# Attention over heads in a six-block network on one Trainium2 core: split real and imaginary parts, gates without matmuls, mixing by features in two token halves

## The chip, the cores and the metric

The program runs on one core of a Trainium2 chip. A core has TensorE (PE in the profile; PEld is its weight loads), VectorE (DVE), ScalarE (ACT), GpSimd (POOL) and SyncE (SP, whose queue starts the DMAs). The metric is device time in microseconds (us); lower is better.

## What is computed

Two levels of three residual blocks (cross attention, attention, feed forward) act on x, 8 x 64 tokens of 512 features. The change touches one of the six: the attention over heads of level 1, between cross attention and experts. In a token its 8 heads attend to each other; there is no attention between tokens. Cut to what matters:

```python
x = x + attn(layernorm(x))
q, k, v = split(query @ W_qkv.T + b_qkv)               # each [B, S, 8 heads, 64]
encode(v) = v / max(norm(v), 1e-12) * exp(1j * phases) # phases: one per feature
for depth in range(3):                                 # on encode(q) and encode(k)
    s1, s2 = state[:, :, :-1], state[:, :, 1:]         # heads i and i + 1
    rot = cos(theta / 2) * s2 + sin(theta / 2) * exp(1j * phi) * conj(s2)
    state = concat([abs(s1)**2 * rot + (1 - abs(s1)**2) * s2, state[:, :, -1:]])
coh = exp(1j * angle(sum(encode(v), heads)))
for c in range(4):                                     # circuits
    pattern = einsum('bsid,bsjd->bsij', conj(qa), ka)  # 8 x 8 in each token
    probs = softmax(abs(pattern)**2 * scale)
    co = einsum('bsij,bsjd->bsid', sqrt(probs + 1e-12), encode(v)) * coh
    final += sup_w[c] * clip(abs(co), 1e-6, 1) * exp(1j * angle(co))
return real(final).reshape(B, S, 512) @ W_out.T + b_out
```

## The kernel before

Everything is one program whose blocks follow one another. Each block is made of stages (class `Stage`, L59), and each stage ends with a barrier over all engines, which the profile lists as L73. In a stage every engine has its own instruction list, in the order written; lists meet only at semaphores. All tensors of this block are fp32, 512 tokens; a PSUM bank holds 512 columns.

`head_attention` (L1708) opens a stage for its long-lived tensors and calls, in this order:

`norm_transpose` (L92): layer norm on VectorE, transposes on TensorE (L192), copies to `xt`. SyncE loads `w_qk` meanwhile (L1737), in which the columns of each head stand twice.

`head_project` (L1749): for each of 16 queries and keys (`u`), four matmuls of 512 columns (L1822) whose 128 output rows are the head's 64 features twice, for the real and the imaginary part; ScalarE adds the bias (L1863) and squares (L1868); a matmul sums the squares over the 64 rows (L1812). Then the values, head by head, 64 rows (L1836), transposed to (head, token) groups (L1842). VectorE inverts the 16 x 512 lengths (L1947), splits them into three bf16 parts (L1951, L1954), TensorE spreads them over the rows (L1851), and VectorE scales the states with them and with the cosine or sine of the phase (L1963). It also builds 21 gate matrices `rot` (L1923, L1926). GpSimd makes the constant matrices first and TensorE waits for them (`made`).

`entangle` (L1970): `units` is 3 depths x 7 gates x (query, key) = 42. For each, ScalarE squares head i (L1991), TensorE adds real and imaginary squares (L2010, matrix `same`) and applies the gate (L2013, matrix `rot`), ScalarE copies the first result (L2000), VectorE multiplies (L2024) and adds (L2026).

`head_scores` (L2031): tokens lie in 32 groups of 16 (`NG`, `GT`). TensorE turns the keys (L2070) and multiplies query group by key group, 128 x 128 (L2063), of which only equal tokens count; VectorE picks these with a mask `own` (L2094) and sums (L2099).

`head_mix` (L2106): softmax on small tensors (L2156 to L2166, exponential L2256, root L2267). Then, for 4 token tiles x 4 circuits in two halves each (`halves`, 32): VectorE or, for each fourth, GpSimd widens the weights to 128 x 128 blocks (L2145), TensorE transposes them (L2312), ScalarE copies (L2281), TensorE multiplies them with the values, 64 columns at a time (L2324). ScalarE takes size and sign (L2274, L2275), VectorE clips and scales (L2174 to L2177), GpSimd adds over the circuits (L2206, L2208) and makes `face` (L2227 to L2240), VectorE applies it (L2183, L2184). At the end the sums are transposed (L2344, L2288), and TensorE makes the output with 8 matmuls of 64 rows and a bias matmul for each token tile (L2353, L2354), VectorE adds it to x (L2197).

## Time and profile before

| | us |
|---|---|
| Median of 3 runs (lowest, highest) | 3393.12 (3390.45, 3395.27) |
| The profiled execution | 3391.88 |
| Its span, first to last instruction | 3390.2 |
| TensorE busy in it | 3130.2 (92%) |
| VectorE busy | 1574.2 (46%) |
| ScalarE busy | 1010.7 (30%) |
| GpSimd busy | 133.7 (4%) |

The profile is of one execution, 1.7 us longer than its span. "Busy" is the time in which an engine executes; TensorE's matmuls are pipelined, so that busy is not the same as at its peak. The clock column (PEclk) is the TensorE clock that was granted, as a share of 2.4 GHz; 0.50 is the lower of its two levels. An fp32 matmul shows as two records. `out<-in` names what an instruction writes and reads; the prefix is the stage (n, hp, he, hs, hm) or `ha` for the tensors of the whole block.

### The profile page before, as it was taken

To read this page: it belongs to the slowest core of one execution; us is meant where nothing else is said; L and a number is where in the kernel's file an instruction comes from. 1 tells how busy PE (TensorE), PEld (TensorE's weight loads), DVE (VectorE), ACT (ScalarE), POOL (GpSimd) and SP (SyncE) were. 2 spreads that over 40 slices of the span, in tenths; PEclk is the share of its full clock that TensorE was granted. 3 is DMA by queue.
4 is the path that set the end of the run, shared out by engine and by line. 5 is a ranking of instruction groups with operands and counts; after the bars stand their busy time and mean duration, and the time that the engine had idled before them with its cause. 6 is when DMAs were issued, how large, how long until landed. Compare 5 with 4: busy or idle time off the path is not lost. (4 is left out here: it accounts for less than half of the span.)

```text
span 3390.2 us, 41575 instructions
## 1 busy us (share of the span) xinstructions
PE 3130.2 (92%) x17509; PEld 1704.9 (50%) x17517; DVE 1574.2 (46%) x1808; ACT 1010.7 (30%) x1527; POOL 133.7 (4%) x239
## 2 busy tenths in 40 slices
PE   6979999959899999899999999999999869779899
PEld 3334444424344444466666666666666523348353
DVE  5359999955532222334343434343333240679110
ACT  3354333313332222223232323232332202344010
POOL 1000000000000000000000000000000000016000
PEclk9989999989999999999999999999999979795599
DMA  5123343333233333445554555455544420000113
GB/s 199 50 78 90 93 140 92 93 138 112 87 112 101 102 100 108 148 95 138 119 141 109 139 119 141 109 137 118 141 112 98 90 94 0 0 13 1 53 47 136
DMA packets 467232, 338.50 MB, mean 100 GB/s; under 512 B 227780, under 2 KB 432901, under 8 KB 462375
## 3 DMA queue, kind: packets, MB, share of 16 engines
q1 hardware_dynamic: 467046, 335.84, 36.0%
q8 instruction: 139, 2.28, 0.3%
q14 instruction: 47, 0.38, 0.0%
HBM read 227.68 MB, written 53.58 MB: 83 GB/s over the span
## 5 line engine op out<-in xcount | busy, mean ns | idle before, releaser
L366 PE MATMUL vw_pv<-vw_wv,vw_ctx 128*128 128x512 f16 (+1 forms) x1296 | 497.0, 384 | 63.0 <-DVE vw_vst L386 27.6
L367 PE MATMUL vw_pv<-vw_wv,vw_ctx 128*128 128x512 f16 (+1 forms) x1296 | 496.9, 383 | 0.0
L368 PE MATMUL vw_pv<-vw_wv,vw_ctx 128*128 128x512 f16 (+1 forms) x1296 | 495.9, 383 | 0.0
L1442 PE MATMUL ca_p_s<-early_halves,ca_qw 128*128 128x448 f16 (+2 forms) x1408 | 467.4, 332 | 1.4 <-DVE ca_qw L1555 1.4
L1443 PE MATMUL ca_p_s<-early_halves,ca_qw 128*128 128x448 f16 (+2 forms) x1408 | 467.4, 332 | 0.0
L1444 PE MATMUL ca_p_s<-early_halves,ca_qw 128*128 128x448 f16 (+2 forms) x1408 | 467.3, 332 | 0.0
L1555 DVE TENSOR_TENSOR ca_qw<-ca_p_w,ca_qw 128x512 f16<-128x512 f32 x128 | 88.5, 691 | 545.6 <-ACT ca_qw L1505 545.6
L386 DVE TENSOR_TENSOR vw_vst<-vw_pv,vw_vst 128x512 f16<-128x512 f32 x162 | 110.7, 687 | 377.1 <-ACT vw_vst L377 377.0
L1505 ACT ACTIVATE ca_qw<-ca_p_w 128x512 f16<-128x512 f32 x128 | 76.4, 597 | 560.5 <-PE ca_p_w L1423 560.5
L366 PEld LDWEIGHTS vw_pv<-vw_wv,vw_ctx 128*128 128x128 f16 (+1 forms) x1296 | 127.8, 99 | 229.3 <-issue 40.4
L377 ACT ACTIVATE vw_vst<-vw_pv 128x512 f16<-128x512 f32 x162 | 95.4, 592 | 468.6 <-PE vw_pv L368 468.6
L1444 PE MATMUL ca_p_s<-ca_ctx,ca_qw 128*128 128x448 f16 (+2 forms) x640 | 215.5, 337 | 0.0
L1443 PE MATMUL ca_p_s<-ca_ctx,ca_qw 128*128 128x448 f16 (+2 forms) x640 | 215.4, 337 | 0.0
L1442 PE MATMUL ca_p_s<-ca_ctx,ca_qw 128*128 128x448 f16 (+2 forms) x640 | 215.4, 337 | 0.0
L368 PEld LDWEIGHTS vw_pv<-vw_wv,vw_ctx 128*128 128x128 f16 (+1 forms) x1296 | 127.8, 99 | 156.8 <-issue 6.5
L367 PEld LDWEIGHTS vw_pv<-vw_wv,vw_ctx 128*128 128x128 f16 (+1 forms) x1296 | 127.7, 99 | 154.5 <-issue 7.7
L1444 PEld LDWEIGHTS ca_p_s<-early_halves,ca_qw 128*128 128x128 f16 x1408 | 138.0, 98 | 99.4 <-issue 0.9
L1442 PEld LDWEIGHTS ca_p_s<-early_halves,ca_qw 128*128 128x128 f16 x1408 | 138.0, 98 | 90.9 <-DVE ca_qw L1555 1.7
L1513 ACT ACTIVATE ca_probs<-ca_p_s,ca_small 128x896 f32<-128x896 f32 (+1 forms) x128 | 117.7, 925 | 220.3 <-DVE ca_small L1564 220.3
L1443 PEld LDWEIGHTS ca_p_s<-early_halves,ca_qw 128*128 128x128 f16 x1408 | 138.0, 98 | 89.1 <-issue 0.7
L1577 DVE SCALAR_TENSOR_TENSOR ca_parts<-ca_probs,ca_small,ca_parts 128x1602 f16<-128x1602 f32 x64 | 120.8, 1888 | 119.1 <-ACT ca_parts L1522 119.1
L873 ACT ACTIVATE work<-early_halves,mb_a_neg 128x252 f32<-128x252 f32 x256 | 104.7, 492 | 218.0 <-DVE ms_h L905 215.4
(405 smaller groups left out, 5126.4 us busy)
## 6 DMA issues: line engine op xcount, KB each, us to landing
vw_ring<-in_ctx_t SPq DMA_DIRECT2D x109, 512.0 KB, 3.7
vd<-vw_vst SPq DMA_DIRECT2D x192, 256.0 KB, 2.3
ca_vals<-vd SPq DMA_DIRECT2D x64, 768.0 KB
ca_stage<-in_ctx_t SPq DMA_DIRECT2D x91, 512.0 KB, 3.5
ex_w_d<-in_w_d SPq DMA_DIRECT2D x8, 2048.0 KB, 7.2
early_r<-state_rows SPq DMA_DIRECT2D x8, 1024.0 KB, 7.5
early_r<-in_w SPq DMA_DIRECT2D x2, 4096.0 KB, 14.2
vw_ring<-in_w_kv SPq DMA_DIRECT2D x8, 512.0 KB, 4.7
```

The lines of the kernel that those rows point to most:

```text
L366: self.nc.tensor.matmul(o, xh[:, c, 0:w], self.wv[0][:, c, f], start=(c == 0), stop=False)
L367: self.nc.tensor.matmul(o, xh[:, c, 0:w], self.wv[1][:, c, f], start=False, stop=False)
L368: last = self.nc.tensor.matmul(o, xl[:, c, 0:w], self.wv[0][:, c, f], start=False, stop=(c == CC - 1))
L377: self.nc.scalar.activation(self.staged(u, 0), self.bank(u).rearrange("p (c n) -> p c n", n=P), ACT.Copy).then_inc(self.vhi, 1)
L386: self.nc.vector.tensor_tensor(self.staged(u, 1), self.bank(u).rearrange("p (c n) -> p c n", n=P), self.staged(u, 0), ALU.subtract).then_i ...
L873: ins = nc.scalar.activation(da[q][:, m, :, 1:], steps, ACT.Exp, scale=a_neg[:, e, q * NQ + m:q * NQ + m + 1])
L1442: nc.tensor.matmul(o, a[:, 0, c, :], x[:, 0, c, lo:hi], start=(c == 0), stop=False)
L1443: nc.tensor.matmul(o, a[:, 0, c, :], x[:, 1, c, lo:hi], start=False, stop=False)
L1444: last = nc.tensor.matmul(o, a[:, 1, c, :], x[:, 0, c, lo:hi], start=False, stop=(c == CC - 1))
L1513: nc.scalar.activation(probs[:, CUTS[2 * h]:CUTS[2 * h + 2]].rearrange("p (a n) -> p a n", a=2), scores(f, h), ACT.Exp, bias=nbias, scale= ...
L1555: nc.vector.tensor_tensor(qw[f % 2][:, 1, c, :], p_w[:, :].rearrange("p (c n) -> p c n", n=P), qw[f % 2][:, 0, c, :], ALU.subtract).then_i ...
L1577: nc.vector.scalar_tensor_tensor(parts[:, 1, 0:KEYS], probs[:, :], rinv, parts[:, 0, 0:KEYS], ALU.mult, ALU.subtract).then_inc(wl_done, 1)
```

## The change

`head_attention` becomes a single stage with one block; `head_project`, `entangle`, `head_scores` and `head_mix` go. Rows of all tensors are now query features (0 to 63) and key features (64 to 127), and real and imaginary part are two tensors. All work up to the pattern is done in two token halves of 256 tokens (`a`), each with its own tensors.

- `w_qk` holds each column once, ordered by head with query and key side by side, so one unit of 8 (`project`) gives query and key of a head; a unit has 256 columns. Length inverses are spread by fp32 matmuls (`spread_norm`).
- The gate is a scaling by a complex number once the state is turned into the frame in which the gate is diagonal: ScalarE squares (`squares`) and makes two factors for each head from the squares (`factors`, scale and bias from `gain` and `base`), VectorE multiplies (`product`) and turns the frame between depths with two scalar_tensor_tensor for each head (`turned`). TensorE has no part in it.
- Values are projected with tokens on the rows (`values`), normalised, stored to a DRAM tensor `v_rows` and read back by (head, token in group) rows into `vz` (`turn`), which GpSimd has cleared. It reuses the space of the weights.
- After the last depth, ScalarE copies and SyncE's DMAs rearrange the halves of the rows into query, key and turned key (`copies`, `move`).
- Scores as before, keys stationary. The softmax over heads is done with heads on the rows: `peaks`, `peaks_back`, `totals`, `totals_back` are small transposes and matmuls between the score units.
- The mixing goes by token group (32): one widening of 512 elements (2 x 4 circuits x 4 head pairs x 16 tokens), two matmuls of 256 columns with `vz` stationary (`mix`). The result has features on the rows. The sum over circuits is taken by matmuls with scaled identities `sup_d` (`total`), 8 for each token tile, one set for the clipped values and one for the squared signs. `faced` applies the phase. Output: four 128-row matmuls and the bias for a tile (`out`), without transposes.

The core of the diff (removed lines and most added ones are left out):

```diff
+            def store(a):
+                for t in (2 * a, 2 * a + 1):
+                    sp.wait_ge(vhat_done, t + 1)
+                    sp.dma_start(io.v_rows[t * P:(t + 1) * P, :], vhat[:, t, :]).then_inc(v_stored, 16)
+            def turn(a):
+                sp.wait_ge(v_stored, 32 * (a + 1))
+                sp.wait_ge(vz_zero, 1)
+                for j in range(NH):
+                    sp.dma_start(vz[j * GT:(j + 1) * GT, a * HG:(a + 1) * HG, DH:2 * DH],
+                                 io.v_rows[a * HN:(a + 1) * HN, j * DH:(j + 1) * DH].rearrange("(g t) d -> t g d", t=GT))\
+                        .then_inc(vz_ready[a], 16)
+            def move(a):
+                sp.wait_ge(s_done, 2 * (2 * (DEPTH - 1) + a + 1))
+                sp.wait_ge(last_head, 2 * a + 2)
+                for out, v, lo in ((query, s_im, 0), (key, s_re, DH), (key_t, s_im, DH)):
+                    sp.dma_start(out[a][DH - lo:2 * DH - lo, :, :, :].rearrange("p g h t -> p (g h t)"),
+                                 v[a][lo:lo + DH, :, :, :].rearrange("p g h t -> p (g h t)")).then_inc(m_dma[a], 16)
+            store(0)
+            turn(0)
+            move(0)
+            store(1)
+            move(1)
+            turn(1)
...
+            def project(a, i):
+                u = a * NH + i
+                if i == 0:
+                    pe.wait_ge(xt_done, 2 * (a + 1))
+                if u >= 3:
+                    pe.wait_ge(sq_done, u - 2)
+                for c in range(DC):
+                    last = nc.tensor.matmul(raw_bank(u), w_qk[:, c, i, :],
+                                            xt[:, c, a * HN:(a + 1) * HN], start=(c == 0), stop=(c == DC - 1))
...
+            def spread_norm(a):
+                pe.wait_ge(inv_done, a + 1)
+                for q in range(NH // 2):
...
+            def score(a, u):
+                m = a * 8 + u
+                if u == 0:
+                    pe.wait_ge(m_dma[a], 48)
+                    pe.wait_ge(m_act, 3 * (a + 1))
+                if m >= 2:
+                    pe.wait_ge(picked_done, m - 1)
+                keys = (key, key_t)[u % 2][a]
+                for g in range(GB):
+                    at = u // 2 * GB + g
+                    last = nc.tensor.matmul(bank(m % 2)[:, g * P:(g + 1) * P], keys[:, at, :, :].rearrange("p h t -> p (h t)"),
+                                            query[a][:, at, :, :].rearrange("p h t -> p (h t)"), start=True, stop=True)
+                last.then_inc(sc_ready, 1)
...
+            def totals(a):
+                pe.wait_ge(e_done, CIRC * (a + 1))
+                for c in range(CIRC):
+                    last = nc.tensor.matmul(bank(2)[:, 2 * P + c * GT:2 * P + (c + 1) * GT], e[:, c, :], own[:, :], start=True,
+                                            stop=True)
...
+            def mix(g):
+                u = g // 2
+                if g % 2 == 0 and u >= 2:
+                    pe.wait_ge(sign_done, 2 * u - 2)
...
+                o = bank(4 + u % 2)[:, g % 2 * HN:(g % 2 + 1) * HN]
+                nc.tensor.matmul(o, vz[:, g, DH:3 * DH], wide[g % 4][:, 0:HN], start=True, stop=False)
+                nc.tensor.matmul(o, vz[:, g, 0:2 * DH], wide[g % 4][:, HN:2 * HN], start=False, stop=True).then_inc(x_ready, 1)
+            def total(t):
+                pe.wait_ge(clip_done, 4 * t + 4)
+                pe.wait_ge(q_done, 4 * t + 4)
+                if t:
+                    pe.wait_ge(y_ready, t)
+                for i, v in enumerate((clipped, unsigned)):
+                    parts = v[t % 2].rearrange("p g h t -> p (g h t)").rearrange("p (g c m t) -> p c m g t", c=CIRC, m=NH // 2, t=GT)
+                    for c in range(CIRC):
+                        last = nc.tensor.matmul(bank(6 + i), sup_d[:, i, c, :], parts[:, c, :, :, :], start=(c == 0),
+                                                stop=(c == CIRC - 1))
+                last.then_inc(t_ready, 1)
...
+            for u in range(8):
+                score(0, u)
+            peaks(0)
+            score(1, 0)
+            score(1, 1)
+            peaks_back(0)
+            score(1, 2)
+            score(1, 3)
+            totals(0)
+            score(1, 4)
+            score(1, 5)
+            totals_back(0)
+            score(1, 6)
+            score(1, 7)
+            pe.wait_ge(vsign_done, 1)
+            pe.wait_ge(diag_done, 2 * CIRC)
             for g in range(NG):
...
+            def factors(a, g):
+                if g == 0:
+                    act.wait_ge(c_done, a + 1)
+                    act.wait_ge(gates_ready, 1)
+                else:
+                    act.wait_ge(rot_done, 2 * (g - 1) + a + 1)
+                for i in range(NU):
+                    m = gate(g, i)
+                    nc.scalar.activation(f_im[a][:, :, i, :], f_re[a][:, :, i, :], ACT.Identity, bias=base[:, 1, m:m + 1],
+                                         scale=gain[:, 1, m:m + 1]).then_inc(f_done, 1)
+                    act.wait_ge(f_done, 2 * NU * (2 * g + a) + 2 * i + 1)
+                    nc.scalar.activation(f_re[a][:, :, i, :], f_re[a][:, :, i, :], ACT.Identity, bias=base[:, 0, m:m + 1],
+                                         scale=gain[:, 0, m:m + 1]).then_inc(f_done, 1)
...
+            def copies(a):
+                act.wait_ge(s_done, 2 * (2 * (DEPTH - 1) + a + 1))
+                act.wait_ge(last_head, 2 * a + 2)
+                lo, hi = slice(0, DH), slice(DH, P)
+                flat = lambda v: v.rearrange("p g h t -> p (g h t)")
+                nc.scalar.activation(flat(query[a][lo, :, :, :]), flat(s_re[a][lo, :, :, :]), ACT.Copy).then_inc(m_act, 1)
+                nc.scalar.activation(flat(key[a][hi, :, :, :]), flat(s_im[a][hi, :, :, :]), ACT.Copy).then_inc(m_act, 1)
+                nc.scalar.activation(flat(key_t[a][hi, :, :, :]), flat(s_re[a][hi, :, :, :]), ACT.Copy,
+                                     scale=-1.0).then_inc(m_act, 1)
...
+            def product(a, g):
+                m = 2 * g + a
+                dve.wait_ge(f_done, 2 * NU * (m + 1))
+                if g == 0:
+                    dve.wait_ge(n_done, 4 * (a + 1))
+                else:
+                    dve.wait_ge(last_set, 2 * a + 2)
+                    c.settle()
+                for s, r, f in ((s_re, r_re, f_re), (s_im, r_im, f_im)):
+                    v = r[a][:, :, FH, :] if g else n[a][:, :, 1:NH, :]
+                    nc.vector.tensor_tensor(s[a][:, :, FH, :], f[a][:, :, FH, :], v, ALU.mult).then_inc(s_done, 1)
+            def turned(a, g):
+                dve.wait_ge(s_done, 2 * (2 * (g - 1) + a + 1))
+                for i in range(NU - 1):
+                    m = rot(g, i)
+                    re, im = s_re[a][:, :, i + 1, :], s_im[a][:, :, i + 1, :]
+                    c.mark(nc.vector.scalar_tensor_tensor(r_re[a][:, :, i, :], im, tan[:, 0, m:m + 1], re, ALU.mult, ALU.add))
+                    c.mark(nc.vector.scalar_tensor_tensor(r_im[a][:, :, i, :], re, tan[:, 1, m:m + 1], im, ALU.mult, ALU.add))
+                dve.wait_ge(c_done, 2 + 4 * (g - 1) + 2 * a + 2)
+                nc.vector.tensor_tensor(f_re[a][:, :, FH, :], f_re[a][:, :, FH, :], f_im[a][:, :, FH, :],
+                                        ALU.add).then_inc(rot_done, 1)
...
+            inverse(0)
+            normed(0)
+            inverse(1)
+            normed(1)
+            product(0, 0)
+            value_sum(0)
+            value_sum(1)
...
+            def widen(g):
+                if g >= 4:
+                    dve.wait_ge(x_ready, g - 3)
+                dve.wait_ge(w_done, CIRC * (g // HG + 1))
+                nc.vector.tensor_tensor(wide[g % 4].rearrange("p (n t) -> p n t", t=GT),
+                                        wt[:, g // HG, g % HG, :, :, :].rearrange("p i c m -> p (i c m)").unsqueeze(2)
...
+            def bound(u):
+                t = u // 4
+                dve.wait_ge(sign_done, 2 * u + 2)
+                if u % 4 == 0 and t >= 2:
+                    dve.wait_ge(t_ready, t - 1)
+                out = clipped[t % 2].rearrange("p g h t -> p (g h t)")[:, u % 4 * BANK:(u % 4 + 1) * BANK]
+                nc.vector.scalar_tensor_tensor(out, size[u % 2], 1e-6, sign[u % 2], ALU.max, ALU.mult).then_inc(bounded, 1)
+                dve.wait_ge(bounded, u + 1)
+                nc.vector.tensor_scalar(out, out, 1.0, -1.0, ALU.min, ALU.max).then_inc(clip_done, 1)
+            def faced(t):
+                dve.wait_ge(t_ready, t + 1)
+                dve.wait_ge(face_done, 1)
+                if t:
+                    dve.wait_ge(y_ready, t)
+                four = lambda v: v.rearrange("p (m t) -> p m t", m=NH // 2)
+                nc.vector.tensor_tensor(four(y_1), four(bank(6)), face[:, t * P:(t + 1) * P].unsqueeze(1)
+                                        .to_broadcast([P, NH // 2, P]), ALU.mult).then_inc(y_half, 1)
+                dve.wait_ge(y_half, t + 1)
+                nc.vector.scalar_tensor_tensor(y_t[:, t, :], bank(7), eps[:, 1:2], y_1, ALU.add, ALU.add).then_inc(y_ready, 1)
...
+            for u in range(17):
+                if u < 16:
+                    widen(2 * u)
+                    widen(2 * u + 1)
+                if u == 1:
+                    peak(1)
+                elif u == 2:
+                    below_peak(1)
+                elif u == 4:
+                    inverse_total(1)
+                elif u == 5:
+                    weigh(1)
+                if u:
+                    bound(u - 1)
+                if u % 4 == 2 and u > 4:
+                    faced(u // 4 - 1)
+                if u % 4 == 0 and u > 4:
...
+    data["w_qk"] = rows(wqkv[:2 * D].T).reshape(P, DC, 2, NH, DH).transpose(0, 1, 3, 2, 4).reshape(P, DC, NH, P)
...
+    io.v_rows = nc.dram_tensor("v_rows", (TOK, D), f32, kind="Internal").ap()
```

## Rows read from the trace of the kernel before

**Rows 1.** Table by stretches: length, busy PE, PEld, DVE, ACT, POOL, clock, DMA share, GB/s.
```profile
2767.90:2782.00 14.10, 3.67 (x16) 3.27 (x16) 6.40 (x16) 1.29 (x3) 2.71 (x12) 0.50 0.86 323
2782.00:2858.60 76.60, 76.07 (x161) 25.91 (x161) 13.41 (x66) 22.73 (x34) 0.00 (x0) 0.96 0.03 10
2858.60:2886.00 27.40, 27.40 (x65) 8.66 (x64) 0.00 (x0) 4.78 (x7) 0.00 (x0) 1.00 0.00 1
2886.00:2927.30 41.30, 23.29 (x81) 8.22 (x80) 26.10 (x34) 6.45 (x10) 0.00 (x0) 0.55 0.00 0
2927.30:3003.30 76.00, 73.84 (x168) 32.48 (x168) 57.95 (x84) 46.95 (x84) 0.00 (x0) 0.98 0.00 1
3003.30:3031.70 28.40, 21.46 (x144) 17.48 (x144) 21.57 (x34) 5.41 (x9) 2.01 (x10) 0.97 0.00 1
3031.70:3043.40 11.70, 5.79 (x8) 2.06 (x8) 7.59 (x7) 9.51 (x12) 3.55 (x2) 0.78 0.40 90
3043.40:3140.80 97.40, 84.13 (x408) 79.19 (x408) 87.52 (x80) 38.31 (x70) 69.81 (x44) 0.54 0.00 1
3140.80:3207.00 66.20, 64.79 (x80) 23.35 (x80) 3.39 (x5) 1.07 (x2) 0.00 (x0) 0.51 0.00 0
```

**Rows 2.** Timeline, TensorE, two units of query-key projection: start, length, engine, line, count.
```profile
2801.99 3.70 PE L1822 MATMUL hp_p_p<-work,hw_w_qk 128*128 128x512 f32 x8
2806.58 3.70 PE L1822 MATMUL hp_p_p<-work,hw_w_qk 128*128 128x512 f32 x8
```

**Rows 3.** Groups of instructions in 2767.9 to 3207.1: busy us, mean ns | idle before.
```profile
L2353 PE MATMUL hm_p_out<-hm_w_o,hm_y_t 64*128 64x512 f32 x64 | 56.0, 1066 | 0.0
...
L2145 DVE TENSOR_TENSOR hm_wide<-hm_wgt,ha_own 128x512 f32<-128x512 f32 x24 | 36.5, 1551 | 4.7 <-ACT hm_wgt L2267 3.0 <-PE hm_p_x L2312 1.7
...
L1836 PE MATMUL hp_p_p<-work,hp_w_v 128*64 128x512 f32 x64 | 27.7, 593 | 0.0
```

**Rows 4.** Timeline, ScalarE: a run of 252-element operations, and two around the root.
```profile
229.64 6.43 ACT L873 ACTIVATE work<-early_halves,mb_a_neg 128x252 f32<-128x252 f32 x16 [2.58 <-PEq L73]
...
3039.10 1.91 ACT L2263 ACTIVATE hm_vsq<-hm_vsign 128x2048 f32<-128x2048 f32 x1
3041.03 1.28 ACT L2267 ACT_TABLE_LOAD   x1
```

**Rows 5.** Groups of instructions, VectorE, of the whole span and of this block.
```profile
L899 DVE TENSOR_TENSOR ms_h<-early_r,ms_du 128x2048 f32<-128x2048 f32 x32 | 73.2, 2288 | 1.5
...
L1926 DVE SCALAR_TENSOR_TENSOR ha_rot<-hp_swap,hp_coef,ha_rot 128x128 f32<-128x128 f32 x21 | 5.6, 344 | 0.0
...
L1947 DVE RECIPROCAL hp_root<-hp_root 16x512 f32<-16x512 f32 x1 | 3.3, 3341 | 0.0
```

**Rows 6.** Timeline, VectorE, picking and summing the scores, 3019.9 to 3022.
```profile
3019.91 0.68 DVE L2094 TENSOR_TENSOR hs_picked<-hs_p_s,ha_own 128x512 f32<-128x512 f32 x1
3020.63 0.69 DVE L2099 TENSOR_REDUCE hs_part<-hs_picked 128x32 f32<-128x512 f32 x1
3021.23 0.68 DVE L2094 TENSOR_TENSOR hs_picked<-hs_p_s,ha_own 128x512 f32<-128x512 f32 x1
```

**Rows 7.** Table by stretches, clock in the gates' first microseconds and in the mixing.
```profile
2931.00:2940.00 9.00, 9.00 (x22) 3.98 (x22) 6.90 (x10) 5.47 (x11) 0.00 (x0) 1.00 0.00 0
3084.00:3094.00 10.00, 9.40 (x46) 9.09 (x45) 9.93 (x10) 4.00 (x8) 7.65 (x6) 0.50 0.01 2
```

**Rows 8.** Timeline, 3057 to 3058, GpSimd and VectorE side by side.
```profile
3057.17 4.51 POOL L2240 TENSOR_TENSOR hm_face<-hm_vsum,hm_vsq 128x2048 f32<-128x2048 f32 x1
...
3057.43 4.81 DVE L2145 TENSOR_TENSOR hm_wide<-hm_wgt,ha_own 128x512 f32<-128x512 f32 x1 [1.13 <-PE hm_p_x L2312]
```

**Rows 9.** Timeline, 3031 to 3036, a GpSimd clearing and VectorE's operation beside it.
```profile
3032.60 1.81 POOL L2212 MEMSET hm_acc<- 128x2048 f32 x1 [25.02 <-POOLq L73]
...
3033.44 2.74 DVE L2159 TENSOR_SCALAR hm_tiny<-ha_sup 128x4 f32<-128x4 f32 x1
```

**Rows 10.** The page's part 3, the DMA queue: packets, MB, share of 16 engines.
```profile
q1 hardware_dynamic: 467046, 335.84, 36.0%
```

1061 lines of the change are left out of this document (515 added, 546 removed).

## The prediction, made before the changed kernel was run

> **What bounds the kernel now.** I read the stage table first [rows 1]: the head attention fills 2767.9 to 3207.0, 439.1 us of the 3390.2 us span, and nothing outside it is edited. The stages are closed by barriers, so each counts in full, and the reader should ask in each which engine is full. TensorE is full while it projects queries and keys (76.07 of 76.60 us), projects values (27.40 of 27.40), runs the gates (73.84 of 76.00) and makes the output (64.79 of 66.20). Only two stages are different: lengths and scaling (41.3 us, TensorE 23.3, VectorE 26.1, in turns) and the mixing (97.4 us, TensorE 84.1, VectorE 87.5, GpSimd 69.8 busy). Second I read the clock column of the same table: the mixing had 0.54 and the output 0.51 of full clock, so 163.6 us ran at about 1.2 GHz. Third, single instructions, for prices [rows 2 to 6].
>
> **Prices.** An fp32 matmul shows as two records. The value projection's 32 matmuls of 512 columns took 27.7 us at full clock, 0.86 us each, the output's 1.7 us at half clock [rows 3]; so 0.43 us per 256 columns at full clock, 0.86 at half. A score matmul of 128 columns is a quarter of 0.86, 0.21. ScalarE: 252 elements with a per-partition scale come at a pitch of 0.40 (16 in 6.43), last 0.49 alone; 2048 take 1.91; a table load 1.28 [rows 4]. VectorE: 2048 elements with two inputs 2.29, a scalar_tensor_tensor of 128 elements comes every 0.27 (21 in 5.6), so 0.40 at 256; reciprocal of 512 elements 3.34 [rows 5]. One of 512 elements I take at 0.60 to 0.62 where the next is free and 0.72 where the next waits for it; a picking pair comes every 1.32 [rows 6].
>
> **Part 1, up to the first projection: 14.1 to 10.1 us.** The norm moves into the one big stage, so the GpSimd constants (before: behind a barrier, made only at 2782) and the small loads start at once, and the query-key weights are 2 MB, not 4: they used to be sent twice, for real and imaginary rows; 4 MB filled the DMA at 323 GB/s in this stretch [rows 1]. VectorE's copy of the turned x now stands behind a wait for the small loads, which queue behind 2 MB; 2 MB at 323 GB/s is 6.2 us from 2769, so 2776, plus copies: 2778. Bounds: 8 to 13 us.
>
> **Part 2, queries and keys: 76.6 to 47.** A unit (four matmuls and the length matmul) came every 4.59 us [rows 2], 16 units. Query and key of a head now share one stationary matrix and a unit has 256 columns: 16 x 2.30 = 36.7. Added inside: transposes of the second half 1.5, the first matmuls at half clock 2.5, the first half's length spreading 8 x 0.43 = 3.4 and the wait for its inverse, of which about 2 is bare (table load 1.3, root 0.4, clamp 0.3, reciprocal 1.7, minus one unit of TensorE that hides it). Sum 46, and 1 for the second root: 47, so the gates begin at 2825. ScalarE needs 0.9 us a unit, hidden. Bounds 43 to 52.
>
> **Part 3, values and gates: 27.4 + 41.3 + 76.0 = 144.7 to 80.** The values (4 x 5 matmuls, 17 us) and the second spreading now lie beside ScalarE's and VectorE's gate work and cost nothing; if that cover were gone they would cost 17 + 3.4. The three-way split of the inverse (4 of the 41.3) is gone. The gates lose 84 matmuls, and this saves almost nothing by itself: VectorE and ScalarE now carry them. Per half and depth: ScalarE one or two squares of 1792 elements (1.7 each) and 7 pairs of 256-element factors, the second of a pair waiting for the first, 0.49 + 0.03 + 0.40 = 0.92 a pair, 6.5; VectorE two products of 1792 (2.0 each) and, from depth 1, 12 turns (4.8) and a sum (2.0). Chained by the written order, from the start of the gates: first product of half 0 done at 12, half 1 at 25 (it waits for its factors, which wait for the second spreading at 13), turns 32 and 38, products 42 and 49, value sums 50, turns 57 and 64, value scaling 67, product 71, value scaling 74, product 78. Behind this lie the moves for half 0: three 64-partition DMAs of 512 KB behind eight DMAs of value rows on SyncE's queue, landing at 80; half 1's copies (3 x 1.9 on ScalarE) and moves hide behind half 0's scores. First scores at 2905. No row shows factors with both scale and bias: below, a pair could cost 0.80 (no exposed wait), above, 1.1; with about five calls on the chain that is -4 to +6. I take 0.92, nearest to the rows. Moves: from 4 us (323 GB/s and 2 of latency) to 12. GpSimd copies and clears here; see below.
> A rule of the Trainium skill speaks against the moves (SBUF — State Buffer, "Door 1: The DMA port swizzle"): 64 partitions of one half reach only half the ports, 196 GB/s against 328. By it 1.5 MB takes 8 us and not 4.7, and the scores start some 3 us later. No row here shows a 64-partition copy of this size.
>
> **Part 4, scores and softmax: 28.4 + 11.7 = 40.1 to 40.** VectorE's picking is unchanged: 16 x 1.32 = 21.1 [rows 6] (TensorE needs 0.9 a unit at full clock and 1.7 to 1.8 cold; it starts cold, +2). The softmax is cut into small steps that TensorE turns forward and back between the scores, in strict order, and there the change adds waits: totals(0) stands on TensorE's queue ahead of score(1,4), waits for a table load and four exponentials (2.9 us), and VectorE, queued for score(1,4), sits idle about 4. In the same way peaks, peaks_back and totals_back cost 1.2, 1.3 and 1.9, and the root's table load 1.1 before the mixing. Steps themselves 5.5, faces 1.1. Sum 21.1 + 2 + 9.5 + 6.6 = 39, say 40. Bounds 35 to 47. Mixing starts at 2945.
>
> **Part 5, mixing and output: 97.4 + 66.2 = 163.6 to 85.** Removed: the transposes of the widened weights, their copies, 128 matmuls of 64 columns, clipping per circuit with two GpSimd accumulators, transposes of the sum, and 64-row output matmuls. New TensorE work at full clock: 64 matmuls of 256 columns 27.4, the weighted sum over circuits 32 of 512 columns 27.4, output 20 of 512 columns 17.1 (128-row contraction, so 4 + bias, not 8 + bias): 72. VectorE: 32 widenings 0.62, 16 bounds 1.1, four times 2.1: 46 and 3 of softmax: 49. ScalarE 16 x 1.7 = 27. GpSimd nothing. So TensorE is the bound, except in the first six units, where VectorE's 2.34 + 2.6/6 exceeds TensorE's 1.71: 15.5. Then 61.7 of TensorE, three small waits for the faced output (1.5), and a tail that nothing hides: signs and bound of the last unit 2.5, faced 1.6, last add 0.8. Sum 83, and 2 while cold: 85. End at 3030.
> What sets the 61.7 is the clock. The gates' 512-column matmuls, on matrices nearly all zero, reached 1.00 in their fourth microsecond and had 0.98 over the stage; the mixing, TensorE 94% busy, stayed at 0.50 [rows 7], and the 64-row output at 0.51 [rows 1]. The new matmuls use all 128 rows and stream 256 or 512 columns, like the gates', so 2.4 GHz; zeros in the widened weights should matter as little as in the gates.
> The Trainium skill says that transposes don't count as TensorE's being busy (TensorE: Matmul & The Clock Gate, "Part 4: PE-mode transpose"). The mixing's 0.50 at 94% busy agrees, but the 64-row output stayed at 0.51 with none; by the rule alone the new loop, without transposes, is at full clock too.
> Port: a VectorE widening took 4.81 us beside a GpSimd operation of 4.51 [rows 8]; the 24 cost 36.5 instead of 15 [rows 3]. All GpSimd work leaves this loop. What remains are four 256-element copies and one clearing of 6144 columns beside products with two inputs; beside a GpSimd clearing a tensor_scalar of 4 elements took 2.74 [rows 9]. I take zero, since no tensor_scalar stands there; at most 5, the clearing's length by 1.81 for 2048 columns in the same rows.
>
> **Sum.** 10 + 47 + 80 + 40 + 85 = 262 against 439: 177 us less. After it the experts' stage is the same; its first transposes may be 1.5 us faster or not. Own time of the profiled run 3391.9 - 177 = 3214.9; it lay 1.2 under the median, so 3216. All spans summed leave no slack for latencies between some 100 small chained steps; only the roundings upward are there for that.
>
> **Rivals.**
> (a) The clock stays at 1.2 GHz in the mixing, since TensorE pauses before it and is only 70% busy in the first units. Price: 72 us again if throughout: 3288; half of it: 3252. For: [rows 7], the old loop never recovered for long. Against: cold, the new loop is TensorE-bound at 3.4 us a unit, 100% busy with full-height matmuls. 9%.
> (b) The ScalarE-VectorE ping-pong of the gates and softmax is dearer: pairs at 1.1, moves and value rows at 12, each exposed wait 0.3 longer over some 60 steps: 20 to 30 us, 3241. For: the value rows go out and back through memory in 2048 pieces of 256 B, and packets cost 36.0% x 16 x 3390 / 467046 = 0.042 us each on average [rows 10], 5 us over 16 engines, more if few engines get them. 14%.
> (c) The stalls of part 4 overlap better and the projection has no exposed waits: 3197. 10%.
> (d) Slower than before: the sums over circuits read their moving operand in 64-byte runs, 1 KB apart. 32 such matmuls cost 27.4; they would have to cost 6.4 us each, 7.5 times as much, for the gain to be gone; at ten times, 3462. Against: half of the gates' matmuls read 64-byte runs too, and that stage's 168 records came every 0.44 us [rows 1], the rate of contiguous ones [rows 3]. 1%.
> (e) It doesn't do what it says: the gates' cost only moves and nothing else is gained. Part 3 grants the first half; the gain then is TensorE's removed columns alone. Halved projection is certain from [rows 2]: 3355. 1%.
>
> **How the numbers follow.** Forecast 65% within 3202 to 3235, (a) 9, (b) 14, (c) 10, (d) 1, (e) 1. The range 3194 to 3256 holds the forecast, most of (b) and (c) and the milder half of (a). About 0.2% (7 us) can be told from no change here: faster 0.98, same 0.005, slower 0.015.
>
> **What would show it.** First projection at 2778; units 2.30 apart; the last gate product ending 78 us after the second root of the key lengths; VectorE idle about 4 us behind totals(0); clock 1.00 from the eleventh group on and sum matmuls at 0.86; widenings at 0.68 with none above 1. Wrong if the clock column of the mixing reads near 0.5, or the gates take over 90 us.

## The result

The changed kernel took 3235.05 us (median of 4 runs, 3228.4 to 3238.93) against 3392.39 us for the kernel before, run beside it: ratio 0.9535, 95% interval 0.9523 to 0.9547, 157 us less. The forecast was 3216 us, 177 us less. The gain is 20 us smaller than forecast; the time lies at the upper edge of what I had given the forecast itself (3202 to 3235), and nearer to rival (b) at 3241 than to the forecast.

The profiled run (3228.4 us, span 3226.7) is the lowest of the four, and its block begins at 2761.1, 6.8 us earlier than in the profile of before, though the two kernels do not differ ahead of the block. So the block is compared by its own length, from its first DMA to the first of the experts' stage: before 2767.9 to 3208.1, 440.2 us (barrier included); after 2761.1 to 3045.4, 284.3 us. That is 155.9 us, the difference of the medians but for 1.4.

The table by stretches of the kernel after answers to [rows 1] (length, busy PE, PEld, DVE, ACT, POOL, clock, DMA share, GB/s):

```profile
2761.10:2772.40 11.30, 1.96 (x9) 1.62 (x9) 6.97 (x23) 0.80 (x2) 2.97 (x13) 0.50 0.83 299
2772.40:2824.30 51.90, 49.40 (x185) 32.20 (x186) 11.35 (x50) 18.71 (x40) 0.73 (x2) 0.89 0.04 17
2824.30:2910.40 86.10, 25.40 (x60) 10.81 (x60) 64.72 (x86) 76.49 (x117) 9.49 (x3) 0.64 0.14 35
2910.40:2951.00 40.60, 25.57 (x142) 23.90 (x142) 26.04 (x44) 9.61 (x14) 0.00 (x0) 0.75 0.27 57
2951.00:3045.40 94.40, 80.51 (x246) 46.04 (x246) 47.25 (x83) 32.52 (x58) 0.00 (x0) 0.97 0.00 0
```

They are the five parts of the prediction: up to the first projection, queries and keys up to the second root, values, gates and moves, scores and softmax, mixing and output. The last row has the largest share of the gain, 69 of the 156 us: [rows 1] had 163.6 us at a clock of 0.54 and 0.51 there, now it is 94.4 us at 0.97. The gates' row has 59 (144.7 to 86.1), the projection's 25 (76.6 to 51.9), and the scores gave nothing.

Where the gain fell short, the timelines show. TensorE in the middle of the second half's projection (start, length, count, idle before):

```profile
2804.30 1.99 PE L1890 MATMUL ha_ps<-work,ha_wreg 128*128 128x256 f32 x8
2806.22 0.60 PE L1897 MATMUL ha_ps<-ha_sqn,ha_pick 128*16 128x256 f32 x2
2808.54 5.61 PE L1907 MATMUL ha_ps<-ha_lengths,ha_spread 16*128 16x256 f32 x16 [1.71 <-DVE ha_lengths L2315]
2814.08 3.69 PE L1890 MATMUL ha_ps<-work,ha_wreg 128*128 128x256 f32 x8
```

A unit takes 2.46 us. Behind a pause of 1.71 us and the 16-row matmuls, one unit takes twice as long: the clock of 2812 to 2816 reads 0.50. The factors on ScalarE, and the last of the moves' DMAs with the first score:

```profile
2895.23 0.59 ACT L2093 ACTIVATE ha_f_im<-ha_f_re,ha_base,ha_gain 128x256 f32<-128x256 f32 x1
2895.85 0.60 ACT L2096 ACTIVATE ha_f_re<-ha_f_re,ha_base,ha_gain 128x256 f32<-128x256 f32 x1
2896.36 0.58 ACT L2093 ACTIVATE ha_f_im<-ha_f_re,ha_base,ha_gain 128x256 f32<-128x256 f32 x1
...
2901.92 1.96 SPq L1839 DMA_DIRECT2D ha_f_re<-ha_s_im  x1
...
2910.45 2.05 PE L1963 MATMUL ha_ps<-ha_r_re,ha_r_im 128*128 128x128 f32 x8 [5.69 <-DMA ha_f_re<-ha_s_im]
```

A pair comes every 1.13 us. VectorE between the scores, and TensorE's first and a later gap in the mixing:

```profile
2926.06 0.69 DVE L2398 TENSOR_TENSOR ha_n<-ha_ps,ha_own 128x512 f32<-128x512 f32 x1 [1.32 <-PE ha_ps L1963]
2930.78 0.69 DVE L2398 TENSOR_TENSOR ha_n<-ha_ps,ha_own 128x512 f32<-128x512 f32 x1 [1.52 <-PE ha_ps L1963]
2939.27 0.69 DVE L2398 TENSOR_TENSOR ha_n<-ha_ps,ha_own 128x512 f32<-128x512 f32 x1 [5.18 <-PE ha_ps L1963]
2945.49 0.69 DVE L2398 TENSOR_TENSOR ha_n<-ha_ps,ha_own 128x512 f32<-128x512 f32 x1 [2.36 <-PE ha_ps L1963]
...
2951.85 1.19 PE L2000 MATMUL ha_ps<-ha_n,ha_wreg 128*128 128x256 f32 x2 [4.70 <-DVE ha_n L2440]
...
2989.71 0.67 PE L2000 MATMUL ha_ps<-ha_n,ha_wreg 128*128 128x256 f32 x2 [1.92 <-DVE ha_n L2440]
```

### The profile page after: what moved, and what is told of

It is laid out like the page before. It is cut to its first block and busy times, and to the rows that moved or that the text cites. A ratio compares the mean times of both kernels' runs of the same rounds, so it can differ in the third digit from the quotient of the medians.

```text
span 3226.7 us, 40186 instructions
## 1 busy us (share of the span) xinstructions
PE 2927.9 (91%) x17021; PEld 1616.3 (50%) x17029; DVE 1506.7 (47%) x1769; ACT 1012.3 (31%) x1525; POOL 68.6 (2%) x189
## 5 line engine op out<-in xcount | busy, mean ns | idle before, releaser
L1555 DVE TENSOR_TENSOR ca_qw<-ca_p_w,ca_qw 128x512 f16<-128x512 f32 x128 | 88.5, 691 | 545.6 <-ACT ca_qw L1505 545.6
```

The costliest lines, as they stand in the source:

```text
L1555: nc.vector.tensor_tensor(qw[f % 2][:, 1, c, :], p_w[:, :].rearrange("p (c n) -> p c n", n=P), qw[f % 2][:, 0, c, :], ALU.subtract).then_i ...
```

## The experiments

Every kernel is the changed one with one edit, but for e6 (which holds e5's edit too) and the last two. The times of one kernel differ by up to 12 us, and in the profiles the block begins anywhere from 2761 to 2768, so single edits are read from the stretches of their profile, in us, cut at the events of the table above (the mixing begins with the first widening):

| run | to projection | queries, keys | gates, moves | scores | mixing, output | block | median time |
|---|---|---|---|---|---|---|---|
| after | 11.3 | 51.9 | 86.2 | 40.6 | 94.4 | 284.3 | 3235.05 |
| e1_half_height | 11.8 | 52.0 | 88.3 | 41.4 | 109.3 | 302.7 | 3249.94 |
| e2_transposes | 11.9 | 51.7 | 86.4 | 40.0 | 106.4 | 296.5 | 3249.06 |
| e3_im_first | 11.6 | 52.1 | 82.7 | 40.8 | 94.4 | 281.6 | 3229.77 |
| e4_totals_late | 11.6 | 51.7 | 86.4 | 33.5 | 94.4 | 277.7 | 3229.06 |
| e5_spread_late | 11.4 | 48.3 | 86.6 | 40.0 | 94.4 | 280.7 | one run |
| e6_spread_full | 11.6 | 46.6 | 86.6 | 41.3 | 98.3 | 284.4 | one run |
| e7_moves_split | 11.2 | 51.9 | 83.0 | 40.7 | 97.8 | 284.6 | one run |
| e8_bounds_late | 11.5 | 51.6 | 86.5 | 40.4 | 97.8 | 287.8 | one run |
| e9_pool_back | 11.9 | 51.4 | 86.5 | 41.5 | 111.5 | 302.9 | 3251.09 |
| e10_short | 11.7 | 52.3 | 88.2 | 41.1 | 146.9 | 340.2 | 3280.08 |
| e11_all | 11.8 | 46.5 | 76.7 | 33.7 | 92.5 | 261.1 | 3209.58 |
| e12_fill | 11.2 | 46.7 | 76.9 | 33.7 | 90.0 | 258.5 | 3205.29 |

A stretch that an edit leaves alone repeats within about 1.5 us, but the gates (86.2 to 88.3) and the mixing, which is 94.4 or about 98 (see e8; it is why e6's and e7's blocks are no shorter than that of the kernel after).

### What holds the clock in the mixing: e10, e2, e1

e10 cuts the mixing matmuls to the 64 columns of the old ones:

```diff
-                nc.tensor.matmul(o, vz[:, g, DH:3 * DH], wide[g % 4][:, 0:HN], start=True, stop=False)
-                nc.tensor.matmul(o, vz[:, g, 0:2 * DH], wide[g % 4][:, HN:2 * HN], start=False, stop=True).then_inc(x_ready, 1)
+                for j in range(0, HN, DH):
+                    nc.tensor.matmul(o[:, j:j + DH], vz[:, g, DH:3 * DH], wide[g % 4][:, j:j + DH], start=True, stop=False)
+                    last = nc.tensor.matmul(o[:, j:j + DH], vz[:, g, 0:2 * DH], wide[g % 4][:, HN + j:HN + j + DH],
+                                            start=False, stop=True)
+                last.then_inc(x_ready, 1)
```

> The mixing matmuls of 256 columns are cut into four of 64 columns each, as in the mixing before (each loads its 128 weight columns anew); sums, output and all else stay. The mixing before came at 0.21 us a record at half clock. Theory that short matmuls, more weight loading than streaming, are what held the clock at 0.54: clock 0.5 all through the first twelve groups, 3.4 us a group, 35 to 41 us for them instead of 19, and the later groups at half clock wherever they stand together: 60 to 80 us more, about 3305. Rival, that the old mixing's pauses held it down: clock 1.00 after some 6 us, a group 1.75 us, 28 us more less what VectorE's waits hid (about 8): 3255.

Its stretches: the first twelve groups; the first sums and outputs with groups between; six groups alone behind the second output; and last, the six groups behind the first output, which lie inside the second row:

```profile
2957.00:3003.00 46.00, 45.31 (x208) 44.46 (x209) 16.55 (x31) 12.53 (x23) 0.00 (x0) 0.50 0.00 1
3003.00:3046.00 43.00, 42.92 (x223) 28.76 (x221) 17.11 (x29) 11.58 (x21) 0.00 (x0) 0.97 0.00 1
3046.00:3065.00 19.00, 19.00 (x89) 18.23 (x88) 5.43 (x10) 4.71 (x9) 0.00 (x0) 0.52 0.00 1
...
3018.60:3029.60 11.00, 10.92 (x97) 10.81 (x97) 5.24 (x9) 3.43 (x6) 0.00 (x0) 1.00 0.01 1
```

TensorE is 98% busy for 46 us and the clock stays at 0.50, where the kernel after, cold too, was at 1.00 from its seventh microsecond on. It rises in the middle of the first 512-column sums and falls again, without a pause, in the six short groups behind the second output. The same six behind the first output ran at 1.00 for 11 us: short groups did not raise the clock here, but they did not bring it down each time either. So the old mixing's 0.54 [rows 1] [rows 7] comes back for the first twelve groups by cutting the matmuls to 64 columns, with neither the old pauses nor the transposes. The cut also gives each 64 columns a weight load of their own (PEld is busy 44.5 of the 46 us); no run separates the two. Median 45 us over the kernel after; I had said 70, because I did not expect the sums to lift the clock, short groups included, for over 40 us. The 45 us hold more than the clock: where it is at 1.00, a short group still takes 1.8 us instead of 0.87. (The profiled run is 7 us over its median.)

e2 puts eight transposes behind each of the last 20 groups' matmuls, a third of TensorE's time:

```diff
+                if g >= 12:
+                    if g == 12:
+                        pe.wait_ge(wn_done, 2)
+                    for i in range(8):
+                        nc.tensor.transpose(bank(3)[:, i % 4 * P:(i % 4 + 1) * P], sup_d[:, 0, i % 4, :], k.ident[:, :])
```

> Behind each of the last 20 groups' mixing matmuls stand 8 transposes of a 128x128 tile, written to a bank that nobody reads: about a third of TensorE's time from there on, as in the mixing before. At full clock they take 1.2 us a group (four took 0.60), 24 us in all. Theory that transposes let the clock fall as the mixing before showed: clock near 0.5 behind the twelfth group, 24 x 2 + 60 us more, about 3340. Rival, that the 64-column matmuls or the waits of the old mixing did it: clock 0.95 to 1.00, 3259 us.

```profile
2984.00:3030.00 46.00, 46.00 (x230) 32.25 (x229) 21.56 (x37) 13.74 (x24) 0.00 (x0) 1.00 0.00 1
```

The clock stays at 1.00. Eight of them took 0.87 us, not 1.2, 17.4 us in all, of which 12.0 show; the rest filled gaps. The prediction cited the Trainium skill's rule that transposes do not count as TensorE's being busy (TensorE: Matmul & The Clock Gate, "Part 4: PE-mode transpose"); at this share among long matmuls the clock stayed at 1.00, and e10 shows that the old mixing's clock needs no transposes to be explained. A loop of transposes alone was not run.

e1 contracts the sums and the output over 64 rows (the upper 64 rows are left out of the sums):

```diff
-                        last = nc.tensor.matmul(bank(6 + i), sup_d[:, i, c, :], parts[:, c, :, :, :], start=(c == 0),
+                        last = nc.tensor.matmul(bank(6 + i), sup_d[0:DH, i, c, :], parts[0:DH, c, :, :, :], start=(c == 0),
-                    nc.tensor.matmul(bank(t % 2), y_t[:, t, m * P:(m + 1) * P], w_o[:, m, :], start=(m == 0), stop=False)
+                    nc.tensor.matmul(bank(t % 2), y_t[0:DH, t, m * P:(m + 1) * P], w_o[0:DH, m, :], start=(m == 0), stop=False)
```

> The contraction of the 32 sum matmuls and of the 16 output matmuls is cut from 128 rows to 64 (the upper 64 rows are left out of the sums); number, columns and order of the matmuls stay. Theory that what the matmuls are made of holds the clock (here, rows used): from the first sum on the granted clock is near 0.5, a pair of records of 512 columns comes every 1.71 us instead of 0.86, and the last 72 us of the stage grow by 45 to 62, to about 3290 us in all; if only the halved matmuls count and the mixing matmuls between them lift the clock again, by half of it, 3262. Rival, that it is enough that TensorE is busy: clock stays 1.00, time 3235 within 10.

Two of its stretches:

```profile
3004.00:3024.00 20.00, 18.07 (x56) 9.89 (x55) 10.13 (x18) 6.23 (x12) 0.00 (x0) 1.00 0.00 0
3040.00:3067.00 27.00, 23.21 (x26) 8.15 (x26) 3.41 (x6) 0.20 (x1) 0.00 (x0) 0.51 0.00 0
```

Its timeline, TensorE, the last sums:

```profile
3040.78 7.19 PE L2011 MATMUL ha_ps<-ha_s_re,ha_spread 64*128 64x512 f32 x8 [2.36 <-DVE ha_s_re L2453]
3047.76 7.03 PE L2011 MATMUL ha_ps<-ha_s_im,ha_spread 64*128 64x512 f32 x8
```

Both theories missed. As long as full-height mixing matmuls stand between, the clock is 1.00 with 64 rows too (2979 to 3040). Behind the last pause (2.36 us) only 64-row matmuls follow, and they run at 0.50 to the end, 27 us. In the kernel after, the same pause is followed by 3.70 us for the 8 records; in e8, where it brought the clock down as well, the 128-row sums had it back at 1.00 within 3.4 us. That tail is 11.3 of the 14.9 us; of the other 3.5, 2.2 lie ahead of the first sum, where this run lost the clock behind `totals(1)`, which the edit does not touch. The tail is what the output before did for 66 us [rows 1] [rows 3].

### The clock in the projection: e5, e6

e5 puts the spreading one unit later (`if i == NH // 2 + 1:`), where the inverse is ready and nothing pauses. e6 does so too, and contracts over 128 rows, 112 of them zeros:

```diff
-                                                sel16[:, i, :, :].rearrange("p s d -> p (s d)"),
-                                                inv[:, a * HN:(a + 1) * HN], start=True, stop=True)
+                                                spread[:, i * P:(i + 1) * P],
+                                                lengths[:, TOK + a * HN:TOK + (a + 1) * HN], start=True, stop=True)
```

> The first half's 8 spreading matmuls (16 rows) stand one unit later, so that the inverse is there and TensorE does not pause for 1.71 us ahead of them. Theory that the 16-row matmuls, back to back, bring the clock down: granted clock 0.5 again right behind them, 3 to 4 us of the 5 stay, and first projection to second root is 50 to 51 us instead of 51.9 (the pause alone is gained). Rival, that the pause brought it down: clock 1.00 throughout, 46.5 to 47.5 us.

> As the run with the spreading one unit later, and the spreading matmuls contract over 128 rows, of which 112 are zeros (GpSimd clears them at the start of the stage), so the result is the same. Theory that the rows used count: clock 1.00 through the spreading, 3.5 us instead of 5.6 for its 16 records, first projection to second root 46.5 to 47.5 us. Rival, that zeros don't count as work or that the pause did it: the clock falls as before, 50 to 52 us. GpSimd's two clearings of 1024 columns may put the first projection back by up to 1 us.

First e5, then e6, the spreading and the unit behind it:

```profile
2811.36 3.97 PE L1907 MATMUL ha_ps<-ha_lengths,ha_spread 16*128 16x256 f32 x16
2815.26 2.91 PE L1890 MATMUL ha_ps<-work,ha_wreg 128*128 128x256 f32 x8
```

```profile
2813.06 3.98 PE L1909 MATMUL ha_ps<-ha_lengths,ha_spread 128*128 128x256 f32 x16
2816.88 1.89 PE L1892 MATMUL ha_ps<-work,ha_wreg 128*128 128x256 f32 x8
```

Without any pause the clock still fell behind the 16-row matmuls (0.57 in 2816 to 2820), later and for less, and 3.6 us were gained, more than I had given the pause. With 128 rows it stayed at 1.00, and 5.3 us were gained, 1.7 of them by the rows. The added rows were zeros and did so all the same. Each is one profile, but the projection of the nine kernels that keep the spreading as it was took 51.4 to 52.3.

### The gates: e3

All seven imaginary factors first, then the real ones; the imaginary product starts at half time.

```diff
-                    act.wait_ge(f_done, 2 * NU * (2 * g + a) + 2 * i + 1)
+                act.wait_ge(f_done, 2 * NU * (2 * g + a) + NU)
+                for i in range(NU):
+                    m = gate(g, i)
...
-                for s, r, f in ((s_re, r_re, f_re), (s_im, r_im, f_im)):
+                for j, (s, r, f) in enumerate(((s_im, r_im, f_im), (s_re, r_re, f_re))):
+                    dve.wait_ge(f_done, 2 * NU * m + (j + 1) * NU)
```

> The imaginary factors of all seven units are made before the real ones, so that none of a pair waits for the other, and the imaginary product starts when its seven factors are done. Theory that the pair's 1.13 us is 2 x 0.50 of pitch and 0.13 of exposed wait: a call of seven pairs 7.0 to 7.2 us instead of 7.9, and the product of 2.0 us runs beside the other seven factors. On the chain of five calls that is 4.5 us, and up to 2 more for each product hidden: the last product ends 6 to 12 us earlier, at 72 to 78 us behind the second root; about 3226 us. Rival, that VectorE's turns and products are the bound of the gates: calls shorter, the last product not more than 2 us earlier, 3235.

```profile
2889.91 3.55 ACT L2093 ACTIVATE ha_f_im<-ha_f_re,ha_base,ha_gain 128x256 f32<-128x256 f32 x7 [2.54 <-DVE ha_f_re L2347]
2893.49 3.55 ACT L2098 ACTIVATE ha_f_re<-ha_f_re,ha_base,ha_gain 128x256 f32<-128x256 f32 x7
```

A pitch of 0.50 for a factor with scale and bias, 7.1 us a call. But the last product ended 4.0 us earlier only (79.6 behind the root, not 72 to 78): from 2880 on VectorE works without a break, and what ScalarE gains turns into its own wait (2.54 above). Each theory holds for a part of the gates.

### The moves: e7

Moves and copies in two parts of eight groups, the first scores behind the first (`gs` is the slice of groups, `m_dma[2 * a + b]` its semaphore).

> The moves to the other 64 partitions and ScalarE's copies are cut into the first and the last eight groups of a half, and the scores of the first eight start when the first three DMAs (0.75 MB) have landed. From the last product of half 0 to the first score it took 9.8 us for 1.5 MB. Theory that this is bytes, 2 us of latency and 7.8 us at 196 to 200 GB/s: first score 3.5 to 4.3 us earlier, at 82 behind the second root, with no new wait at the fifth unit. Rival, that it is issue time on SyncE's queue (0.5, 0.6, 2.0 us) and queueing behind the value rows' packets: first score at most 1 us earlier, or a wait of 2 us or more at the fifth unit.

```profile
2910.64 2.04 PE L1968 MATMUL ha_ps<-ha_r_re,ha_r_im 128*128 128x128 f32 x8 [2.49 <-ACT ha_r_im L2128]
```

The first score is 3.2 us earlier (83.0 behind the root, where I had said 82 and 3.5 to 4.3), and none waits at the fifth unit: it is mostly bytes, though SyncE also had the first three DMAs issued 1.3 us sooner behind the product. The row names ScalarE's copy, but the three copies that the score waits for were done at 2908.5; what it waited for was a DMA. In the kernel after, the stretches from 2901 to 2910 read 198, 213 and 202 GB/s with the DMA engines 92 to 97% busy, against 299 at 83% for the weights above. The prediction weighed the rule of the Trainium skill (SBUF — State Buffer, "Door 1: The DMA port swizzle"): 196 GB/s for 64 partitions. The trace agrees; 1.57 MB at 200 GB/s are 7.9 of the 9.8 us seen.

### The scores: e4

On VectorE, `choose(1, 6)` moves ahead of `inverse_total(0)` to match.

```diff
-            totals(0)
             score(1, 4)
             score(1, 5)
-            totals_back(0)
+            totals(0)
             score(1, 6)
             score(1, 7)
+            totals_back(0)
```

> totals(0) stands behind score(1,5) instead of ahead of score(1,4), and totals_back(0) behind score(1,7). Theory that VectorE's 5.18 us behind totals(0) is TensorE's strict order alone: that idle time falls under 1 us, the 2.36 us behind totals_back(0) goes too and 1 to 2 us come back before the roots; the score stage is 35 us instead of 40.6, and the time 3230. Rival, that VectorE waits for the exponentials' result anyway a little later: the wait moves to the reciprocals of the totals, stage 39 to 41, time unchanged at 3235.

```profile
2937.91 0.68 DVE L2398 TENSOR_TENSOR ha_n<-ha_ps,ha_own 128x512 f32<-128x512 f32 x1
...
2941.45 0.69 DVE L2398 TENSOR_TENSOR ha_n<-ha_ps,ha_own 128x512 f32<-128x512 f32 x1 [0.81 <-PE ha_ps L1963]
...
2943.70 0.68 DVE L2398 TENSOR_TENSOR ha_n<-ha_ps,ha_own 128x512 f32<-128x512 f32 x1
```

5.18 and 2.36 us of waiting became 0.81; the scores are 7.1 us shorter, and no new wait took it back. Two positions in TensorE's order cost more than any other thing that a single run took away.

### The mixing's gaps and GpSimd: e8, e9

e8 holds back `bound` of the last unit but one of a tile behind two widenings.

> Where a group of sums or outputs lets TensorE run four mixing matmul pairs back to back, VectorE widens the next two groups before it bounds the signs of the unit but one, instead of behind it. Theory that the three gaps of 1.92, 1.93 and 2.36 us ahead of a mixing matmul or sum are VectorE's written order, it waits for signs while TensorE waits for a widening: the first two gaps fall under 0.3 us, and widenings' start to the next stage is 90.5 us instead of 94.4. Rival, that VectorE or ScalarE is short of time there: the waits move to the sums, 94 us again.

```profile
2995.89 0.67 PE L2000 MATMUL ha_ps<-ha_n,ha_wreg 128*128 128x256 f32 x2 [1.93 <-DVE ha_n L2440]
3016.62 0.67 PE L2000 MATMUL ha_ps<-ha_n,ha_wreg 128*128 128x256 f32 x2 [1.93 <-DVE ha_n L2440]
3037.76 5.40 PE L2011 MATMUL ha_ps<-ha_s_re,ha_spread 128*128 128x512 f32 x8 [2.36 <-DVE ha_s_re L2453]
```

A miss: the gaps are as before. The timeline shows that VectorE waits in them for the signs of the unit after the one I had moved, and then adds to x; e11 moves these two, and the gaps go. But the run shows something else: behind the same pauses the clock is at 0.50 from 3018 to 3021 and again from 3038.5 to 3042 (5.40 instead of 3.70 for the sum), and the stretch is 97.8, not 94.4. In e7, which leaves the mixing alone, it fell at the same two places, in e6 at others, in the kernel after at none.

e9 gives GpSimd two additions of 512 columns a unit, on tensors that nobody reads any more.

> GpSimd gets two additions of 512 columns a unit beside the mixing, 32 in all, as the two sums that it made in the mixing before (1.3 to 1.5 us each there); nobody waits for them and their result is unused. Theory of the shared port: VectorE's widenings and bounds and GpSimd's additions take turns; where before a widening beside GpSimd took up to 4.81 us, each of the 32 widenings costs 0.5 to 1 us more, VectorE goes from 47 to 65 us and over, TensorE waits for widenings, and the mixing and output grow by 5 to 20 us, 3240 to 3255. Rival, that the widening of before was long for reasons of its own: widenings stay at 0.68, time 3235.

```profile
L1875 POOL TENSOR_TENSOR ha_vhat<-ha_vhat 128x512 f32<-128x512 f32 x32 | 44.8, 1400 | 146.9 <-PE ha_ps L2008 145.5
L2447 DVE TENSOR_TENSOR ha_n<-ha_lengths,ha_own 128x512 f32<-128x512 f32 x32 | 34.3, 1113 | 0.0
```

Widenings at 1.113 us on average, 0.684 in the kernel after; 17.1 us more in the mixing, 16 in the median. So the contention of [rows 8] is real. The 17 us are not its direct price alone: TensorE now waits up to 3.95 us for a widening inside the mixing, and behind such waits its clock is at 0.50 in four stretches, 20 us in all, one of them this:

```profile
2969.60:2976.40 6.80, 6.80 (x22) 5.62 (x21) 6.70 (x8) 2.50 (x6) 4.26 (x4) 0.50 0.00 0
```

### All together: e11, e12

> All together: imaginary factors first, totals(0) behind score(1,5), spreading one unit later and over 128 rows, moves and copies in two parts, and VectorE's order in the mixing mended at the right unit (the gap stands behind the bound of the last unit of a token tile and the addition to x, which now come behind the next two widenings). By the single runs: 5.3 us in the projection, 4.0 in the gates, 3.1 at the moves, 7.0 in the scores, and 3.8 if the two gaps of 1.93 go: stage 261 us instead of 284.3, time 3212. Rival, that one gain eats the other (the gates are bound by VectorE at their end, the mixing by the weights of the first half): stage 266 to 270, 3219.

261.1 us and 3209.58 (ratio to before 0.9467, 0.9453 to 0.948), to 3 us what the single runs said: 5.4 in the projection, 9.5 for gates and moves (the singles gave 3.5 and 3.2; what the rest comes from was not looked for), 6.9 in the scores and 1.9 in the mixing. There the two gaps, 3.85 us together, are gone, but the clock was lost once, 0.51 from 2948 to 2955, behind a pause of 1.96 us at `totals(1)`. e12 fills that pause and the one ahead of the mixing:

```diff
+            def fill(n):
+                for i in range(n):
+                    nc.tensor.matmul(bank(7), k.ident[:, :], w_o[:, i, :], start=True, stop=True)
```

> As the kernel with all five edits, and TensorE multiplies where it would wait: two matmuls of 128 rows and 512 columns into a bank that nobody reads ahead of the first mixing matmul (pause 3.86 us) and two ahead of totals(1) (pause 1.96 us, behind which the clock fell to 0.5 for 7 us). Theory that the pauses alone bring the clock down and that work of any kind at full height and length holds it: clock 0.95 or more from the first mixing matmul to the last output, widenings' start to the next stage 87 to 88.5 us instead of 91.3, stage 257.5, time 3206. Rival, that the fall comes from the short matmuls of totals(1) (16 columns) or that the fillers delay the totals: clock falls again, 91 us or more, 3210.

e11 and then e12 at `totals(1)`:

```profile
2947.52 1.46 PE L1986 MATMUL ha_ps<-ha_own,ha_f_im 128*128 128x16 f32 x8 [1.96 <-ACT ha_f_im L2194]
2948.82 1.20 PE L2007 MATMUL ha_ps<-ha_n,ha_wreg 128*128 128x256 f32 x2
```

```profile
2946.19 1.88 PE L1985 MATMUL ha_ps<-ha_w_o,ident 128*128 128x512 f32 x4
2948.31 1.06 PE L1992 MATMUL ha_ps<-ha_own,ha_f_im 128*128 128x16 f32 x8 [0.25 <-ACT ha_f_im L2202]
2949.23 0.68 PE L2013 MATMUL ha_ps<-ha_n,ha_wreg 128*128 128x256 f32 x2
```

With the filler at `totals(1)` the clock stays at 1.00 (in one profile; the kernel after kept it behind a pause of 1.60 there without one). The one ahead of the mixing does not (0.57 in 2935 to 2939; 2.14 us of pause are left behind it). The mixing takes 90.0 us. My 91.3 for e11 and 87 to 88.5 for this run were counted from the third widening, 1.2 us behind the first; counted so, e12 has 88.8, a little over the range. 3205.29 us (0.9449, 0.9436 to 0.9462), the lowest median of all, though against e11 (5 runs each, 3205.6 to 3217.8 and 3203.2 to 3208.3) the 4 us of the medians are within their spread; the block's 2.6 us are from one profile each.

## Why the prediction was right, and what it missed

**Part 1**, forecast 10.1 and 2778: 11.3, 1.2 late. **Part 2**, 47: 51.9. The unit was mis-sized, 2.46 for 2.30, 2.6 us over 16: I had halved 4.59, but that holds ten times 0.43 and 0.3 that doesn't halve; five times 0.43 and the same 0.3 is 2.45. The rest is the clock, which the forecast had at full speed behind the first matmuls: e5 and e6 show that the spreading's 16 rows and the pause ahead of it (1.71) cost 5.3 us, of which only a pause of 2 was forecast. The two make 5.9 of an excess of 4.9, so the other terms were 1 us too large together.

**Part 3**, 80: 86.1. The step that failed is the price of a pair, 0.92 for 1.13, with about five calls of seven pairs on the chain. I took the scale-only rows [rows 4], 0.49 for one, for scale and bias together, which take 0.59; the bias adds 0.10 to each. The upper bound was 1.1, with +6 for it; it was +5.6 at the last product (83.6 for 78). Here a page had the price: the Trainium skill (ScalarE: Activation LUTs, "What ACT_TABLE_LOAD costs") gives 186 ns, 0.833 ns an element and 93 ns for each per-partition operand, an estimate of 0.585 for 256 elements with both, and the trace has 0.59. The moves, "landing at 80" 9 us behind the product, took 9.8 (e7). ScalarE and VectorE share the bound as the chain had it (e3). GpSimd's clearing took 5.22 us and the products beside it 2.02 and 2.03, so that it cost nothing, as taken; its small copies took 2.13 and 2.19, and the product beside them 2.22, 0.2 more.

**Part 4**, 40: 40.6, with the stalls where they were forecast: 5.18 for 4 behind `totals(0)`, 1.32, 1.52, 2.36 for 1.2, 1.3, 1.9. The mechanism was right (e4). That the sum was right too is in part luck: these four took 10.4 us for 8.4, and the other terms came out 1.4 smaller.

**Part 5**, 85: 94.4. The step on the clock was right in its value (1.00, sums at 0.86, widenings at 0.684), and was worth most: [rows 1] had 163.6 us at half clock in its place, and e10 brings half clock back. What was too small: the cold start (TensorE at 0.50 up to 2957, first sum 19.8 us behind the first widening, not 17.5); the gaps of 1.92 and 1.93 us behind an output, which the forecast had as 1.5 in all (e11: gone); 0.1 to 0.2 us at each change of operand, about 2 by my estimate; and the barrier of 1.4, which lay outside my sum. The sum's own terms make 85.6, and six units at 2.34 + 2.6/6 make 16.6, not 15.5. My reason for the clock, full height and 256 or 512 columns, has more behind it than when it was argued: e10 for the columns (or the weight loads that come with them), e1's tail and e6 for the rows.

**The rivals.** (a), the clock, did not happen, but the pauses that I gave as its reason do bring the clock down in some executions, at 1.7 us a time (e7 and e8: 3.4 us for two). (b) was half of it: pairs at 1.1 and slower moves, some 6 us; the forecast was 3216 and (b) 3241, and the time is nearer to (b), 6 us from it and 19 from the forecast. That it lies inside the range is owed to the range reaching over (b). (c)'s better overlap did not come by itself; e11 and e12 wrote it by hand and went to 3205. (d): the sums' 512-column pairs, with 64-byte runs, came every 0.86 us, 3.43 for four, so strides cost nothing. (e): the gates' cost moved, as said. The sum had no slack, as the prediction noted itself. The 22 us by which the block is over its 262 are the items above, nearly all in three parts: 4.9 in the projection, 6.1 in the gates, 9.4 in the mixing and output.

## What to carry to other kernels

Where TensorE is fully busy at half clock, try its work in other sizes before removing any: here the same twelve groups, both times from a cold start, reached full clock with 256 columns and stayed at half with 64, and 112 rows of zeros made a 16-row step and the unit behind it faster. When an operation's operands differ from the row that prices it, here a bias beside a scale, price the operand. A small matmul with a long wait in a strict order costs what is queued behind it; move it by one or two units.
